# Moving the output projection of a Mamba-2 chunk behind the next chunk's head loop

## The chip, the cores and the metric

The program runs on all 8 cores of one Trainium2 chip. Each core computes half of one of four sequences, and the cores exchange nothing. The metric is the device time of the slowest core in microseconds (us); lower is better. Engines are named as in the profile: PE is TensorE (its matmuls; PEld its weight loads), DVE is VectorE, ACT is ScalarE, POOL is GpSimd and SP is SyncE. A "q" behind a name (POOLq) stands for the part of an engine that issues DMA transfers. TensorE's clock has two levels, 1.2 and 2.4 GHz; the profile prints the granted clock as 0.50 and 1.00.

## The reference

One transformer layer on `x` of shape (4, 4096, 1024): a layernorm, then a Mamba-2 block with a gated feed-forward network behind it, and beside them a second feed-forward network with integer weights, all added to `x`. What matters here is the Mamba-2 mixer and its output projection:

```python
def step(h, inputs):
    dA_t, dt_t, B_t, x_t, C_t = inputs
    dBx = jnp.einsum('bh,bn,bhp->bhpn', dt_t, B_t, x_t)
    h = h * dA_t[:, :, None, None] + dBx
    y = jnp.einsum('bhpn,bn->bhp', h, C_t)
    return (h, y)
_, ys = jax.lax.scan(step, h0, (tm(dA), tm(dt), tm(Bm), tm(x), tm(Cm)))
y = jnp.moveaxis(ys, 0, 1) + D[None, None, :, None] * x
y = y.reshape(b, l, D_INNER)
y = rmsnorm(y * jax.nn.silu(z), ssm_norm_w)
return jnp.einsum('ble,de->bld', y, out_proj_w)
```

There are 32 heads of 64 columns (2048 in all) and a state of 128.

## The kernel before

Each core works through its 2048 tokens in phases, with a barrier between them. Phase A normalises and transposes the tokens. `phase_B` projects and convolves. `phase_C` is the state recurrence in chunks of 128 tokens. It runs twice: `phase_C(1)` carries the state over the preceding half of the sequence and gives no output; `phase_C(0)` does the core's own half and is where the change acts. Phases E and F are the two feed-forward networks.

The order of the work is the order in which `self.op` is called: each call appends one instruction to the list of its engine, with the semaphore values that it waits for. An engine works its list in order, so an instruction that waits holds up everything behind it on the same engine. Semaphores are counted: `sv` by DVE, `st` by PE, `sa` by ACT and `sg` by POOL.

In `phase_C(0)` the 16 rounds of the loop over `ch` (line 792) do this:

- `stageA(ch + 1)` and `bcast_chain(ch + 1)` prepare the decay factors of the next chunk. The chain writes them to device memory and reads them back, spread over all partitions, on SP's queue.
- Sixteen transposes bring x to `x_tok`, and one brings B to `B_tok` (lines 807 to 815). PE transposes, and DVE copies out.
- `vxw` (line 816), on DVE, scales `x_tok` into `xw`.
- `emit_tail(ch - 1)` (line 820) is the output projection of the chunk before. It is 32 matmuls of 128x512 from `ynT` and `wout` into the PSUM tile P1 (line 689), then on DVE the addition of the residual, `h_t<-P,xn_t` (line 697, `ev_o`), and on POOL the transfer of the result to device memory (line 703).
- `mg` and `Gm` (lines 822 and 828) and the `zmm` matmuls (line 833) with `ez`, `y_acc<-P,pt` (line 840), begin the chunk's own output.
- The head loop (lines 846 to 881) does for each of 32 heads a DVE subtraction (`Est`, 855), an ACT exponential (861), a DVE product (`Emt`, 870) and one PE matmul of 64 columns (876) into P0.
- `ev_y` (line 883) adds P0 to `y_acc` on DVE. `tD` (line 886) is the product D * x on POOL, `cscr<-x_tok,c_dexp`; its results are added to `y_acc` by `ev_y2` (line 890) on DVE.
- The state update follows: four matmuls into P0 (line 905, `smm`), `c1` (914) and `t_carry` (919) on DVE. POOL fetches `sz_t` (line 924). Then come the gate (930), the norm (935 to 944) and sixteen transposes of `yn` to `ynT` (line 949), which the next tail reads.

The last chunk's tail is emitted behind the loop, at line 959. One detail of the order carries weight below: POOL's list in a round is the transfer of line 703, then `tD`, then the transfer of line 924. The transfer at line 703 waits for `ev_o`:

```python
t_h1_sp[cc] = self.op("gpsimd", ..., wait=[("sv", ev_o)], ...)
tD = self.op("gpsimd", ..., wait=[("sv", t_xtok), ("sa", t_endB[ch - 1][1])], ...)
ev_y2 = self.op("vector", ..., wait=[("sv", ev_y), ("sg", tD)], ...)
```

Of the kernel before, what the change touches and what calls it, by code (L numbers as in the profile page):

```python
# [55 lines left out]
def ts(i, n=128):  # L56
    return slice(i * n, (i + 1) * n)


class B:  # L60
# [542 lines left out]
    def phase_C(self, stream):  # L603
        import os as _os
        pre = stream == 1
# [69 lines left out]
        t_p0v = None  # L675
# [5 lines left out]
        pend_tail = {}  # L681

        def emit_tail(cc):
            nonlocal t_xn_pv
            ynt_c, ldxn_c = pend_tail.pop(cc)
            omm_c = None
            for f in range(16):
                for q in range(2):
                    omm_c = self.op("tensor", lambda e, f=f, q=q: e.matmul(  # L689
                        P1[:, q * 512:(q + 1) * 512], ynT[:, f * 128:(f + 1) * 128],  # L690
                        wout[:, f * DM + q * 512:f * DM + (q + 1) * 512],
                        start=(f == 0), stop=(f == 15)),
                        wait=([("sv", ynt_c), ("dw", self.t_wo),
                               ("sv", t_xn_pv)]
                              if f == 0 and q == 0 else []),
                        inc=("st", 1) if f == 15 and q == 1 else None)
            ev_o = self.op("vector", lambda e: e.tensor_tensor(
                h1_t[:, :], P1[:, 0:1024], xn_t[:, :], ALU.add),
                wait=[("st", omm_c), ("dh%d" % (cc % 2), ldxn_c),
                      ("dn%d" % ((cc - 1) % 2), t_h1_sp.get(cc - 1))],  # L700
                inc=("sv", 1))
            t_xn_pv = ev_o
            t_h1_sp[cc] = self.op("gpsimd", lambda e, cc=cc: e.dma_start(
                self.h1_dram[ts(cc), :], h1_t[:, :]),
                wait=[("sv", ev_o)], inc=("dn%d" % (cc % 2), 16))
# [86 lines left out]
        for ch in range(NCH):  # L792
# [14 lines left out]
            for f in range(16):  # L807
# [8 lines left out]
            vxw = self.op("vector", lambda e, dw=dw_: e.tensor_tensor(  # L816
                xw[:, :], x_tok[:, :], exp64(dw), ALU.mult),
                wait=[("sv", A["vdw"]), ("sv", t_btok)], inc=("sv", 1))
            if not pre and (ch - 1) in pend_tail:
                emit_tail(ch - 1)  # L820
            if not pre:
                mg = self.op("tensor", lambda e, W0=W0: e.matmul(
                    slotB_f[:, 0:128], xbc[:, 16 * CW + 3 + W0:16 * CW + 3 + W0 + Q],
# [22 lines left out]
                for hh in range(NH + 2):  # L846
# [18 lines left out]
                    if hh >= 2:  # L865
# [14 lines left out]
                                                 if h == 0 else []),  # L880
                            inc=("st", 1))
                t_mt_last = t_mth[NH - 1]
                ev_y = self.op("vector", lambda e: e.tensor_tensor(
                    y_acc[:, :], y_acc[:, :], P0[:, :], ALU.add),
                    wait=[("st", t_mt_last), ("sv", ez)], inc=("sv", 1))
# [7 lines left out]
                t_ya = ev_y2  # L893
                if self.dev_phase is not None:
# [5 lines left out]
                    t_ya = ("so", tdmp)  # L900
            else:
                t_ya = None
            smm = None
            for q in range(4):
                smm = self.op("tensor", lambda e, q=q: e.matmul(
                    P0[:, q * 512:(q + 1) * 512], B_tok[:, :],
                    xw[:, q * 512:(q + 1) * 512], start=True, stop=True),
                    wait=([("sv", vxw)] +
                          ([(t_ya if isinstance(t_ya, tuple) else ("sv", t_ya))]
                           if not pre else [("sv", t_p0v)])  # L910
                          ) if q == 0 else [],
                    inc=("st", 1) if q == 3 else None)
            t_smm = smm
# [8 lines left out]
            t_p0v = t_carry  # L922
# [488 lines left out]
```

How the kernel before makes its waits and increments, by code:

```python
        def run(e, fn=fn, waits=waits, inc=inc):  # L103
            for sn, v in waits:
                e.wait_ge(sems[sn], v)
            inst = fn(e)
            if inc is not None and inst is not None:
                inst.then_inc(sems[inc[0]], inc[1])
# [3 lines left out]
    def wait(self, eng, semname, val):  # L112
        if val:
            sems = self.sems
            self.emits[eng].append(lambda e, sn=semname, v=val: e.wait_ge(sems[sn], v))
```

## Time and profile before

| what | us |
| --- | --- |
| time of the kernel, median of 2 runs | 4405.84 |
| the two runs | 4354.16 and 4457.51 |
| the profiled execution's own time | 4357.55 |
| its span, slowest core (core 2) | 4356.0 |
| spans of all cores | 4345.9 to 4356.0 |
| DVE busy over the span | 1838.4 (42%) |
| PE busy over the span | 2288.3 (53%) |
| POOL busy over the span | 155.6 (4%) |

The profiled execution is one run; its time and its span differ by 1.6 us, so work outside the span plays no part. All durations below come from this execution, on core 2. Rows of the timeline give the start in us, the length in us, the engine, the line and the operation as out<-in; in brackets stands how long the engine was idle before it, and whose result ended that idle time.

### The profile page before, as it was taken

Reading aid. Unit: us, or ns where it says so; the run is one execution under the profiler, and the core shown is the slowest. Engines: PE = TensorE matmul, PEld = TensorE weight load, DVE = VectorE, ACT = ScalarE, POOL = GpSimd, SP = SyncE. Lnnn points to the kernel's source line nnn. Section 1 sums busy time; section 2 is a strip of 40 time slices with the busy share of each in tenths; the row PEclk is TensorE's granted clock in tenths of the full one; section 3 lists DMA queues with packets and bytes.
Section 4 is the critical chain, followed back from the end, with each engine's and each line's share of the span. In section 5 each row is a group of like instructions: output and inputs, shape, how many; then the busy total and the mean of one; then the engine's idle time right before and its main releaser. Section 6 shows DMA issues by size and latency. Waiting matters only on the chain.

```text
span 4356.0 us, 36502 instructions; the slowest of 8 cores (4345.9 to 4356.0 us)
## 1 busy us (share of the span) xinstructions
PE 2288.3 (53%) x9681; PEld 1024.3 (24%) x9681; DVE 1838.4 (42%) x3928; ACT 557.7 (13%) x1011; POOL 155.6 (4%) x160
## 2 busy tenths in 40 slices
PE   0536323435664334343434334777767746788777
PEld 0212111212222111121111111333333313333333
DVE  3533675655515576767666641222222201222222
ACT  3000110000113121212121210111111100000000
POOL 0110000000010000000000000000000000000000
PEclk9998665557877555555555557788887878889988
DMA  6552100011031411111111138000000093111111
GB/s 169 186 162 65 28 0 1 1 38 26 1 77 39 92 64 39 64 44 59 49 54 49 54 70 134 20 20 20 20 20 20 15 151 76 34 34 51 34 34 37
DMA packets 94289, 234.09 MB, mean 54 GB/s; under 512 B 23984, under 2 KB 26832, under 8 KB 93456
## 3 DMA queue, kind: packets, MB, share of 16 engines
q0 software_dynamic: 40448, 106.44, 11.1%
q1 hardware_dynamic: 51344, 116.94, 8.7%
q10 hardware_dynamic: 2304, 8.39, 0.5%
q8 instruction: 91, 1.49, 0.1%
q14 instruction: 102, 0.84, 0.1%
HBM read 235.13 MB, written 51.66 MB: 66 GB/s over the span
## 4 chain that ended last, share of the span: by engine, by line
PE 44%; DVE 23%; issue 14%; DMA 12%; ACT 5%; DVEq 1%; another core or an unknown queue 1%; SPq 0%; ACTq 0%; POOL 0%; POOLq 0%
PE P L1083 4%; PE P L1246 4%; PE P L1250 4%; PE P L689 3%; PE P L478 3%; PE P L483 3%; PE P L1087 3%; DVE Emt L870 3%; DMA bcast<-lam_dram 2%; PE P L1286 2%; PE PS L659 2%; PE P L1125 2%; PE PS L1286 2%; PE PS L1125 2%; DMA wbuf<-w_in 2%
## 5 line engine op out<-in xcount | busy, mean ns | idle before, releaser
L876 PE MATMUL P<-x_tok,Emt 128*128 128x64 bf16 x512 | 108.4, 212 | 328.9 <-DVE Emt L870 328.1
L430 DVE SCALAR_TENSOR_TENSOR B_acc<-xbc,c_convw,B_acc 128x2048 bf16<-128x2048 bf16 x108 | 245.3, 2345 | 0.0
L861 ACT ACTIVATE Est<-Est 128x128 f32<-128x128 f32 x512 | 155.6, 309 | 521.6 <-DVE Est L855 520.1
L1268 DVE TENSOR_TENSOR F_h<-F_h,P 128x1024 bf16<-128x1024 bf16 x48 | 58.6, 1221 | 386.9 <-ACT F_h L1262 386.9
L1105 DVE TENSOR_TENSOR E_h<-E_h,P 128x1024 bf16<-128x1024 bf16 (+1 forms) x48 | 53.3, 1110 | 383.6 <-ACT E_h L1099 383.6
L855 DVE TENSOR_SCALAR Est<-bcast,lam_tok 128x128 f32<-128x128 f32 x512 | 184.8, 366 | 52.1 <-DMA bcast<-lam_dram 2.1
L332 PE MATMUL P<-c_identf,A_n 128*128 128x128 f32 x256 | 90.5, 445 | 196.7 <-DVE A_n L320 165.0
L1246 PE MATMUL P<-wg,F_xf 128*128 128x512 bf16 x384 | 149.1, 388 | 84.1 <-ACT F_h L1262 42.1
L478 PE MATMUL P<-xfh,wbuf 128*128 128x512 bf16 x288 | 115.0, 399 | 144.9 <-DVE wbuf L454 125.6
L1083 PE MATMUL P<-wg,E_hnT 128*128 128x512 bf16 x384 | 146.6, 405 | 82.2 <-ACT E_h L1099 61.3
L870 DVE SCALAR_TENSOR_TENSOR Emt<-Est,dtk,Gm 128x128 bf16<-128x128 f32 x512 | 175.8, 346 | 8.2 <-PE P L876 5.9
L492 DVE TENSOR_TENSOR xbc<-P,r1bc 128x1024 bf16<-128x1024 f32 x72 | 88.3, 1227 | 201.9 <-PE P L483 201.9
L478 PE MATMUL P<-xf,wbuf 128*128 128x512 bf16 x288 | 112.1, 389 | 109.5 <-DVE wbuf L454 109.5
L1125 PE MATMUL P<-wd,E_h2t 128*128 128x512 bf16 x352 | 152.9, 434 | 19.0 <-DMA wd<-w_d 10.2
L1286 PE MATMUL P<-wd,F_h3t 128*128 128x512 bf16 x336 | 146.0, 435 | 27.1 <-DMA wd2b<-w_d 18.4
L1246 PE MATMUL P<-wu,F_xf 128*128 128x512 bf16 x384 | 149.3, 389 | 20.5 <-DMA wu<-w_u 20.5
L1083 PE MATMUL P<-wu,E_hnT 128*128 128x512 bf16 x384 | 140.6, 389 | 23.3 <-DMA wu<-w_u 23.3
L1262 ACT ACTIVATE F_h<-P 128x1024 bf16<-128x1024 f32 x48 | 49.2, 1024 | 805.4 <-PE P L1250 805.4
L1125 PE MATMUL PS<-wd,E_h2t 128*128 128x512 bf16 x352 | 152.1, 432 | 0.0
L1250 PE MATMUL P<-wu,F_xf 128*128 128x512 bf16 x384 | 149.1, 388 | 0.0
L1250 PE MATMUL P<-wg,F_xf 128*128 128x512 bf16 x384 | 149.1, 388 | 0.0
L876 PEld LDWEIGHTS P<-x_tok,Emt 128*128 128x128 bf16 x512 | 53.3, 104 | 390.2 <-issue 390.2
(197 smaller groups left out, 4286.1 us busy)
## 6 DMA issues: line engine op xcount, KB each, us to landing
bcast<-lam_dram SPq DMA_DIRECT2D x64, 512.0 KB
A_x<-x_own SPq DMA_DIRECT2D x32, 512.0 KB, 4.2
A_x<-x_pre SPq DMA_DIRECT2D x32, 512.0 KB, 4.1
wd<-w_d POOLq DMA_DIRECT2D x2, 5376.0 KB, 65.3
wg<-w_g POOLq DMA_DIRECT2D x5, 2048.0 KB, 43.7
wu<-w_u POOLq DMA_DIRECT2D x5, 2048.0 KB, 49.7
xn_dram<-A_n POOLq DMA_DIRECT2D x16, 512.0 KB, 4.8
xfh<-xfp_dram SPq DMA_DIRECT2D x4, 2048.0 KB, 14.2
```

The costliest lines, as they stand in the source:

```text
L430: e.scalar_tensor_tensor(a[:, :], xbc[:, ec * CW + k:ec * CW + k + T], self.c["convw"][:, ec * 4 + k:ec * 4 + k + 1], a[:, :], ALU.mult, A ...
L478: [e.matmul(sl[:, 0:512], self.wbuf[:, dc * 1184 + cr: dc * 1184 + cr + 128], r[:, 0:512], start=(dc == 0), stop=(dc == NDC - 1)), e.matmu ...
L483: e.matmul(sl[:, 512:1024], self.wbuf[:, dc * 1184 + cr: dc * 1184 + cr + 128], r[:, 512:1024], start=(dc == 0), stop=(dc == NDC - 1))][-1],
L855: e.tensor_scalar(est[q3][:, :], bc[g % 2][:, (h % 8) * 128:(h % 8 + 1) * 128], lt[:, h:h + 1], CLAMP, ALU.subtract, ALU.min),
L861: t_ee[h] = self.op("scalar", lambda e, q3=q3: e.activation(est[q3][:, :], est[q3][:, :], AF.Exp), wait=[("sq", gq + 1) if lastg else ("sv ...
L870: e.scalar_tensor_tensor(emt[q][:, :], est[q3][:, :], dk[:, h:h + 1], Gm[:, :], ALU.mult, ALU.mult),
L876: t_mth[h] = self.op("tensor", lambda e, h=h, q=q: e.matmul(P0[:, h * 64:(h + 1) * 64], emt[q][:, :], x_tok[:, h * 64:(h + 1) * 64], start ...
L1083: e.matmul(slots[j][:, 0:512], hnTt[p][:, dc * 128:(dc + 1) * 128], w[:, dc * INTER1 + cb:dc * INTER1 + cb + min(cn, 512)], start=(dc == 0 ...
L1125: mm = self.op("tensor", lambda e, k=k, q=q, pb=pb, kp=kp: e.matmul(pb[:, 0:512], h2t[0:kp, k * 128:(k + 1) * 128], wd1[0:kp, k * DM + q * ...
L1246: e.matmul(slots[j][:, 0:512], xft[p][:, dc * 128:(dc + 1) * 128], w[:, dc * INTER2 + cb:dc * INTER2 + cb + 512], start=(dc == 0), stop=(d ...
L1250: e.matmul(slots[j][:, 512:1024], xft[p][:, dc * 128:(dc + 1) * 128], w[:, dc * INTER2 + cb + 512:dc * INTER2 + cb + 1024], start=(dc == 0 ...
L1286: wt=wsrc[0], kk=wsrc[1]: e.matmul(pb[:, 0:512], h3t[:, k * 128:(k + 1) * 128], wt[:, kk * DM + q * 512:kk * DM + (q + 1) * 512], start=(k ...
```

## The change

It does two things in `phase_C(0)`.

1. The call of `emit_tail(ch - 1)` goes from its place behind `vxw` to behind the head loop, just ahead of `ev_y`. This concerns 15 of the 16 tails; the last one stands behind the loop as before.
2. The four `smm` matmuls wait for `ev_y` in place of `ev_y2`.

Nothing else is edited. Line numbers fall by two behind the first place, are the old ones again from `ev_y` (883) on, and fall by one behind line 905.

```diff
@@ -816,8 +816,6 @@
             vxw = self.op("vector", lambda e, dw=dw_: e.tensor_tensor(
                 xw[:, :], x_tok[:, :], exp64(dw), ALU.mult),
                 wait=[("sv", A["vdw"]), ("sv", t_btok)], inc=("sv", 1))
-            if not pre and (ch - 1) in pend_tail:
-                emit_tail(ch - 1)
             if not pre:
@@ -880,6 +878,8 @@
                 t_mt_last = t_mth[NH - 1]
+                if (ch - 1) in pend_tail:
+                    emit_tail(ch - 1)
                 ev_y = self.op("vector", lambda e: e.tensor_tensor(
                     y_acc[:, :], y_acc[:, :], P0[:, :], ALU.add),
                     wait=[("st", t_mt_last), ("sv", ez)], inc=("sv", 1))
@@ -906,8 +906,7 @@
                     wait=([("sv", vxw)] +
-                          ([(t_ya if isinstance(t_ya, tuple) else ("sv", t_ya))]
-                           if not pre else [("sv", t_p0v)])
+                          ([("sv", ev_y)] if not pre else [("sv", t_p0v)])
                           ) if q == 0 else [],
```

On DVE, between the transposes of a chunk and its head loop, this stood before (`x_tok`, `B_tok` and `xw` are the chunk's inputs, `h_t` is the tail's addition, the numbers behind names are buffers):

```order
L663 COPY B_tok<-PT 128x128
L816 TENSOR_TENSOR xw<-x_tok,dtw_70 128x2048
L697 TENSOR_TENSOR h_t<-P,xn_t 128x1024
L828 TENSOR_TENSOR Gm<-PT,c_triu_b 128x128
L840 TENSOR_TENSOR y_acc<-P,pt_72 128x2048
L855 TENSOR_SCALAR Est_104<-bcast_102,lam_tok_62 128x128
```

And at the same place on DVE in the changed kernel:

```order
L663 COPY B_tok<-PT 128x128
L816 TENSOR_TENSOR xw<-x_tok,dtw_71 128x2048
L826 TENSOR_TENSOR Gm<-PT,c_triu_b 128x128
L838 TENSOR_TENSOR y_acc<-P,pt_73 128x2048
L853 TENSOR_SCALAR Est_104<-bcast_102,lam_tok_63 128x128
```

The tail's addition is gone from here, and `Gm` follows `xw` directly. It now stands on DVE at the end of the head loop, between the last `Emt` and `ev_y`:

```order
L868 SCALAR_TENSOR_TENSOR Emt_108<-Est_105,dtk_74,Gm 128x128
L697 TENSOR_TENSOR h_t<-P,xn_t 128x1024
L883 TENSOR_TENSOR y_acc<-y_acc,P 128x2048
L890 TENSOR_TENSOR y_acc<-y_acc,cscr 128x2048
L913 TENSOR_TENSOR cscr<-Hst,gam_66 128x2048
L918 TENSOR_TENSOR Hst<-cscr,P 128x2048
L929 TENSOR_TENSOR y_acc<-y_acc,sz_t 128x2048
```

`ev_y` and all that comes behind it on DVE now stand behind an instruction that waits for the 32 matmuls. On PE, at the end of the head loop, the changed kernel has these 32 matmuls between the last head (line 874) and the state update:

```order
L874 MATMUL P<-x_tok,Emt_107 128x64
L874 MATMUL P<-x_tok,Emt_108 128x64
L689 MATMUL P<-wout,ynT 128x512 x32
L905 MATMUL P<-xw,B_tok 128x512 x4
L659 MATMUL PS<-c_ident,yn 128x128
```

Before, the 32 stood ahead of the chunk's `mg` (line 822), and line 905 came directly behind the last head. On POOL the changed kernel's list reads, in each chunk:

```order
L703 DMA h_dram<-h_t 128x1024
L886 TENSOR_TENSOR cscr<-x_tok,c_dexp 128x2048
L923 DMA sz_t<-sz_dram 128x2048
```

This is the same list as before. Nothing moved on POOL, but the first of the three waits for the tail's addition, which now comes at the other end of the head loop.

## Rows read from the trace of the kernel before

**Rows 1.** Span and mean granted clock of the slowest core
```profile
core 2: 4356.0 us, clock 0.733
```

**Rows 2.** Waits, 1511 to 2594 us: total us, times, longest us
```profile
DVE h_t L697 <- PE PT L822: 97.3, 15, 7.1
...
PE P L905 <- DVE y_acc L890: 76.1, 15, 5.1
```

**Rows 3.** Timeline, one chunk from the tail into the head loop
```profile
2012.46 8.86 PE L689 MATMUL P<-wout,ynT 128*128 128x512 bf16 x32
2012.78 2.29 DVE L816 TENSOR_TENSOR xw<-x_tok,dtw 128x2048 bf16<-128x2048 bf16 x1
...
2021.56 1.23 DVE L697 TENSOR_TENSOR h_t<-P,xn_t 128x1024 f32<-128x1024 f32 x1 [6.49 <-PE PT L822]
2022.70 0.28 DVE L828 TENSOR_TENSOR Gm<-PT,c_triu_b 128x128 bf16<-128x128 f32 x1
2022.90 2.28 DVE L840 TENSOR_TENSOR y_acc<-P,pt 128x2048 f32<-128x2048 f32 x1
2023.34 0.54 POOL L703 DMA_DIRECT2D h_dram<-h_t  x1 [66.48 <-DVE Gm L828]
2023.89 4.06 POOL L886 TENSOR_TENSOR cscr<-x_tok,c_dexp 128x2048 f32<-128x2048 bf16 x1
2025.10 3.41 DVE L855 TENSOR_SCALAR Est<-bcast,lam_tok 128x128 f32<-128x128 f32 x3
2027.89 0.59 POOL L924 DMA_DIRECT2D sz_t<-sz_dram  x1
...
2028.63 0.35 DVE L870 SCALAR_TENSOR_TENSOR Emt<-Est,dtk,Gm 128x128 bf16<-128x128 f32 x1
```

**Rows 4.** Timeline, the same chunk from its last head on
```profile
2049.28 0.21 PE L876 MATMUL P<-x_tok,Emt 128*128 128x64 bf16 x1 [0.34 <-DVE Emt L870]
2049.67 2.29 DVE L883 TENSOR_TENSOR y_acc<-y_acc,P 128x2048 f32<-128x2048 f32 x1 [0.53 <-PE P L876]
2052.13 2.29 DVE L890 TENSOR_TENSOR y_acc<-y_acc,cscr 128x2048 f32<-128x2048 f32 x1 [0.17 <-DVE y_acc L883]
...
2054.57 1.87 PE L905 MATMUL P<-xw,B_tok 128*128 128x512 bf16 x4 [5.08 <-DVE y_acc L890]
...
2056.93 2.29 DVE L919 TENSOR_TENSOR Hst<-cscr,P 128x2048 f32<-128x2048 f32 x1
2059.13 2.28 DVE L930 TENSOR_TENSOR y_acc<-y_acc,sz_t 128x2048 f32<-128x2048 f32 x1
```

**Rows 5.** Timeline, chunk 0, which has no tail ahead of its head loop
```profile
1445.54 4.04 POOL L886 TENSOR_TENSOR cscr<-x_tok,c_dexp 128x2048 f32<-128x2048 bf16 x1 [18.98 <-DVE x_tok L663]
...
1446.23 5.50 DVE L816 TENSOR_TENSOR xw<-x_tok,dtw 128x2048 bf16<-128x2048 bf16 x1
...
1451.65 0.28 DVE L828 TENSOR_TENSOR Gm<-PT,c_triu_b 128x128 bf16<-128x128 f32 x1
1451.85 2.27 DVE L840 TENSOR_TENSOR y_acc<-P,pt 128x2048 f32<-128x2048 f32 x1
...
1454.89 0.35 DVE L870 SCALAR_TENSOR_TENSOR Emt<-Est,dtk,Gm 128x128 bf16<-128x128 f32 x1 [0.18 <-ACT Est L861]
```

**Rows 6.** Windows: from:to us, length, busy us (count) by engine, granted clock (PEclk), DMA
```profile
2012.40:2016.00 3.60, 3.54 (x9) 1.31 (x10) 2.52 (x2) 0.00 (x0) 0.00 (x0) 0.50 0.00 0
2016.00:2021.20 5.20, 5.20 (x26) 2.30 (x24) 0.00 (x0) 0.00 (x0) 0.00 (x0) 0.99 0.00 0
...
2026.00:2048.00 22.00, 6.14 (x29) 3.01 (x29) 18.49 (x62) 9.42 (x31) 2.48 (x2) 0.51 0.29 97
```

**Rows 7.** Line 924, from issue of the transfer to its landing
```profile
DMA to landing us min/median/max: 3.5/3.9/10.7
```

**Rows 8.** Timeline, weight loads of line 905 at the low clock
```profile
2054.95 0.15 PEld L905 LDWEIGHTS P<-xw,B_tok 128*128 128x128 bf16 x1 [0.28 <-issue]
2055.38 0.15 PEld L905 LDWEIGHTS P<-xw,B_tok 128*128 128x128 bf16 x1 [0.28 <-issue]
```

## The prediction

> **What bounds the kernel now.** I read the span of the cores first: 4356.0 us on the slowest, beside an own time of 4357.55 [rows 1]. Next I read the waits of the second recurrence phase. One wait of DVE belongs to the change: the tail's addition (line 697) stands idle for 97.3 us in 15 chunks, 6.49 us in each [rows 2]. Its releaser is printed as the transpose slot of line 822; that matmul is only the next on PE behind the 32 matmuls of the tail, so the tail is what ends the wait. Then I followed one chunk on the timeline [rows 3, 4]. The reader is to see that DVE sets the pace on both sides of the head loop: `xw`, the wait for the tail, `h_t`, `Gm`, `y_acc`, then the heads, then five operations of 2.3 us each, one behind the other. PE and POOL matter only where DVE waits for them. So the sum is kept on DVE: what each place adds to or takes from its chain, per chunk, times 15. Chunk 0 has no tail ahead of its heads and shows what the freed place looks like [rows 5]; it stays as it is, and so does the last tail behind the loop.
>
> **A, the old place (a gain).** From the end of `xw` (2012.78 + 2.29 = 2015.07) to the start of `Gm` (2022.70) pass 7.63 us [rows 3]: 6.49 idle and 1.14 from the addition's start to the next. In chunk 0 `xw` ends at 1451.73 and `Gm` starts at 1451.65, 0.08 earlier [rows 5]. Gain 7.71 us. `Gm` and `y_acc` need their matmuls (lines 822 and 833), five in all; without the tail they run while DVE is in `xw`, as in chunk 0, so nothing new is late here.
>
> **B, the start of the head loop (a gain).** From the start of `y_acc` at line 840 to the first `Emt` pass 5.73 us in the chunk shown (2022.90 to 2028.63) and 3.04 in chunk 0 (1451.85 to 1454.89) [rows 3, 5]. The difference lies in the first three `Est`, which take 3.41 us together and end just after POOL's product D * x (2023.89 + 4.06 = 2027.95) [rows 3]. In chunk 0 the product runs beside `xw`, and there `xw` takes 5.50 us in place of 2.29 [rows 5, 3]: some DVE operations stand still until POOL's ends, while `y_acc`, which reads PSUM, takes 2.28 beside it as without it [rows 3, 5]. With the change the product leaves the head loop (see D). Gain 2.69 us.
>
> The Trainium skill (SBUF — State Buffer, section "SBUF: two separate sides") says that VectorE and GpSimd share a port pair that one instruction holds to its end, against VectorE operations in a two-port mode or with two SBUF inputs. By that rule the trace agrees: 5.50 against 2.29 us for `xw`, and an unhindered 2.28 for `y_acc` with its PSUM input. Without the rule B would be 0, which is a rival below.
>
> **C, the new place (a cost).** `ev_y` starts 0.39 us after the start of the last head's matmul now (2049.28 to 2049.67) [rows 4]. In the changed kernel PE goes from that matmul to the 32 of the tail, and DVE has nothing to do meanwhile but to wait, since `h_t` stands ahead of `ev_y` in its list. The step to the first of the 32 lies between 0 and the 0.21 us of the head's matmul; I take 0.1. From the first of the 32 to the start of `h_t` pass 9.10 us (2012.46 to 2021.56), and 1.14 more to the next DVE operation [rows 3]. That is 10.34 in place of 0.39: a cost of 9.95 us. The 2.3 us of cover that `xw` gave the tail is lost; that is why the same wait comes back longer than it was.
>
> The 9.10 us hold 3.6 us at a granted clock of 0.50 (1.2 GHz) and then about 1.0 (2.4 GHz) [rows 6]. The tail of now starts at the low level, behind the transposes, and the head loop's 22 us are at 0.51 as well [rows 6], so the new tail starts at the same level. I keep 9.10. The longest of the 15 idle times is 7.1 against the mean of 6.49 [rows 2], so 0.6 us per tail either way is an ordinary spread: 9 us in all. The far bound is a tail at the low level throughout: a matmul each 0.43 us [rows 8] gives 32 x 0.43 = 13.8 us.
>
> The Trainium skill (TensorE: Matmul & The Clock Gate, section "What's actually happening") says that the throttled state is the default and activity releases it. The rows agree in that both the transposes and the heads leave the clock at 0.50 and the dense run lifts it. By that rule the 32 matmuls lift it in the new place too, and the sum is as I have it.
>
> **D, the product on POOL (a cost that the diff doesn't show).** POOL's list is as before, but its first entry, the transfer of line 703, waits for `h_t`. The product stands behind it, and `ev_y2` waits for the product. Counted from the start of `h_t`: the transfer begins after 1.78 us (2023.34), the product after 2.33 (2023.89), and it ends after 6.39 (2027.95) [rows 3]. DVE takes some 0.15 to wake (its own hand-over at line 890 took 0.17 [rows 4]): `ev_y2` at 6.54. Without the wait `ev_y` would start after 1.14, and `ev_y2` 2.46 later (2049.67 to 2052.13) [rows 4]: at 3.60. Cost 2.94 us. Now the product hides in the head loop; its cover is gone. `ev_y` reads PSUM, so by B's rows it isn't slowed beside the product. The bounds of D are 0, if the product were done in time, and 4.06, its whole length.
>
> Queued behind the product is `sz_t` (line 924). It is issued as the product ends, 6.33 us after the start of `h_t` (2027.89), and lands 3.9 us later [rows 3, 7], at 10.2. The gate at line 930 needs it 7.00 us after `ev_y2` starts (2052.13 to 2059.13) [rows 4], at 13.5. That leaves 3.3 us, so it costs nothing. The transfer of `xn_t` for the next tail comes almost a chunk early.
>
> **E, the earlier wait of `smm`.** Its four matmuls wait for `ev_y2` now, 5.1 us in each chunk [rows 2]. But they run 2054.57 to 2056.44, beside `c1`, and line 919, which needs them, starts at 2056.93 when `c1` is done [rows 4]. The wait was hidden. With the edit they run beside `ev_y2` or its wait: worth 0, between 0 and the 0.1 us in which DVE passes from one to the next.
>
> **Sum.** Costs 9.95 + 2.94 = 12.89; gains 7.71 + 2.69 = 10.40; net 2.49 us slower per chunk, x 15 = 37 us. On the profiled execution's own 4357.55 that is 4395 us, 0.9% more. The median shown, 4405.84, is the middle of two runs, 4354.16 and 4457.51; the profiled execution lies at the faster, and my number is of that kind. About 2%, or 87 us, is what a measurement of this kernel can tell from no change.
>
> **The rivals.**
> 1. The product stays hidden, and the kernel isn't slower. If POOL had the product done by the time `ev_y` ends, D would be 0 and the sum -0.45 per chunk: 4351 us. For it: the product's inputs are ready a whole head loop earlier, and POOL was idle for 66.48 us [rows 3]. Against it: POOL takes its list in order and the transfer ahead of it waits for `h_t`. It decides if the product ends over 2.5 us sooner than I count.
> 2. The clock stays low, and the kernel is slower by over 2%. The heads leave PE with 6.14 us of work in 22 [rows 6], less than transposes do. If the tail then ran at the low level to its end it would take 4.7 us more, 15 x 4.7 = 70: 4465 us. It decides from a tail of some 12.4 us on, where 15 x 3.3 brings the loss to 87. Against it: 9 matmuls at the low level sufficed before [rows 6].
> 3. `sz_t` is late. With the longest landing seen, 10.7 us [rows 7], it would be there at 17.0 and the gate wait 3.5 us: 15 x 3.5 = 52, 4447 us, 2.1% slower. Against it: the median is 3.9, and it needs over 7.2 to cost anything.
> 4. B isn't paid back, because the first `Est` are slow for another reason than the product (a transfer, say). Then 40 us are missing: 4435 us. Against it: three `Est` end with the product, and chunk 0 has them fast.
>
> **How the numbers follow.** I give the forecast 0.68, and the rivals 0.12, 0.06, 0.08 and 0.06. The range runs from 4345, rival 1 less the spread of the tails, to 4450, which takes in rivals 3 and 4; only a tail at the low level lies outside. Faster by over 2% needs 87 us, more than any case gives: 0.02. Slower by over 2% is rival 2 and about half of rival 3, with a little for two costs at once: 0.12. The rest, 0.86, is within 2%.
>
> **What would show it.** In the changed profile the wait of `h_t` should be for line 689 and about 9.2 us (15 times, some 140 us in all), with no idle time between `xw` and `Gm`. The first three `Est` should take 0.7 to 0.9 us. `ev_y2` should show a new wait of 2.9 us on POOL, and the chunk should have grown by 2.5 us. I am wrong if a tail takes over 12 us, if the wait for POOL is missing, if `Est` stays at 3.4, or if a wait on `sz_t` shows at the gate.

## The result, and the profile after

The changed kernel is slower by 1.1%: the ratio of its time to the time before is 1.011, with a 95% interval of 1.0057 to 1.0163. Its profiled execution took 4412.81 us against 4357.55, 55.3 us more. The median over all its runs, 4441.53 us, and the 4359.99 of the kernel before hold runs in which one die's clock was lower, so the ratio, which leaves these out, and the two profiled executions are what the text compares.

The spans of the changed kernel's cores, beside [rows 1]:

```profile
core 0: 4411.2 us, clock 0.725
...
die 0 (median of its cores): 4395.2 us, clock 0.725
die 1 (median of its cores): 4400.4 us, clock 0.727
```

The old place, in one chunk on core 0, beside [rows 3] (start us, length us, engine, line, operation):

```profile
2040.15 2.29 DVE L816 TENSOR_TENSOR xw<-x_tok,dtw 128x2048 bf16<-128x2048 bf16 x1
...
2042.35 0.28 DVE L826 TENSOR_TENSOR Gm<-PT,c_triu_b 128x128 bf16<-128x128 f32 x1
2042.63 2.29 DVE L838 TENSOR_TENSOR y_acc<-P,pt 128x2048 f32<-128x2048 f32 x1
2044.84 0.67 DVE L853 TENSOR_SCALAR Est<-bcast,lam_tok 128x128 f32<-128x128 f32 x3
2045.69 0.35 DVE L868 SCALAR_TENSOR_TENSOR Emt<-Est,dtk,Gm 128x128 bf16<-128x128 f32 x1 [0.18 <-ACT Est L859]
```

`Gm` follows `xw` with no idle time, and the first three `Est` take 0.67 us in place of 3.41. Both gains are there. The new place, the same chunk, beside [rows 4]:

```profile
2066.64 0.21 PE L874 MATMUL P<-x_tok,Emt 128*128 128x64 bf16 x1 [0.34 <-DVE Emt L868]
2066.98 9.21 PE L689 MATMUL P<-wout,ynT 128*128 128x512 bf16 x31
...
2076.44 1.23 DVE L697 TENSOR_TENSOR h_t<-P,xn_t 128x1024 f32<-128x1024 f32 x1 [9.95 <-PE P L689]
2077.58 2.28 DVE L883 TENSOR_TENSOR y_acc<-y_acc,P 128x2048 f32<-128x2048 f32 x1
2078.22 0.54 POOL L703 DMA_DIRECT2D h_dram<-h_t  x1 [70.16 <-DVE h_t L697]
2078.77 4.07 POOL L886 TENSOR_TENSOR cscr<-x_tok,c_dexp 128x2048 f32<-128x2048 bf16 x1
2080.00 1.02 PE L905 MATMUL P<-xw,B_tok 128*128 128x512 bf16 x4 [3.81 <-DVE y_acc L883]
2082.77 0.59 POOL L923 DMA_DIRECT2D sz_t<-sz_dram  x1
2082.93 2.29 DVE L890 TENSOR_TENSOR y_acc<-y_acc,cscr 128x2048 f32<-128x2048 f32 x1 [3.08 <-POOL cscr L886]
2085.33 2.29 DVE L913 TENSOR_TENSOR cscr<-Hst,gam 128x2048 f32<-128x2048 f32 x1
2087.73 2.29 DVE L918 TENSOR_TENSOR Hst<-cscr,P 128x2048 f32<-128x2048 f32 x1
2089.93 2.28 DVE L929 TENSOR_TENSOR y_acc<-y_acc,sz_t 128x2048 f32<-128x2048 f32 x1
```

TensorE's clock over the last heads and over the two parts of this tail (from:to us, length, then busy us and counts of PE, PEld, DVE, ACT and POOL, the granted clock, and DMA):

```profile
2050.00:2066.00 16.00, 5.05 (x24) 2.51 (x24) 13.03 (x47) 7.23 (x24) 0.00 (x0) 0.50 0.27 101
2067.00:2071.70 4.70, 4.70 (x12) 1.65 (x13) 0.00 (x0) 0.00 (x0) 0.00 (x0) 0.54 0.19 68
2071.70:2076.60 4.90, 4.44 (x20) 1.86 (x19) 0.16 (x1) 0.00 (x0) 0.00 (x0) 1.00 0.00 0
```

DVE now stands idle for 9.95 us ahead of `h_t`, and for 3.08 us ahead of line 890, where the profile names POOL's product. From `ev_y2` to the gate pass 7.00 us (2082.93 to 2089.93) as before, so neither `sz_t` nor the state matmuls hold anything. The waits of the phase in sum (total us, times, longest), beside [rows 2]:

```profile
DVE h_t L697 <- PE P L689: 162.6, 16, 10.5
...
PE P L905 <- DVE y_acc L883: 57.1, 15, 3.8
DVE y_acc L890 <- POOL cscr L886: 46.4, 15, 3.3
```

The 16 waits of `h_t` include the last tail behind the loop; before, the 15 inner ones were 97.3 us. Worked out from the starts of these DVE operations on core 0 of either trace, as means over chunks 1 to 14:

| place on DVE | before | changed | difference | forecast |
| --- | --- | --- | --- | --- |
| A: start of `xw` to start of `Gm` | 9.87 | 2.21 | -7.66 | -7.71 |
| B: start of `y_acc` to first `Emt` | 5.73 | 3.06 | -2.67 | -2.69 |
| head loop, first to last `Emt` | 20.07 | 20.17 | +0.10 | 0 |
| C: last `Emt` to start of `ev_y` | 0.88 | 11.61 | +10.73 | +9.95 |
| D: start of `ev_y` to `ev_y2` | 2.46 | 5.37 | +2.91 | +2.94 |
| a whole chunk, `xw` to `xw` | 71.27 | 74.80 | +3.53 | +2.49 |

15 x 3.53 is 53 us of the 55. (The five places add up to 3.41; the last 0.1 lies between the start of `Gm` and the start of `y_acc`, 0.31 us in place of 0.20, and its cause is open.)

### The profile page after: what moved, and what is told of

Its sections match the earlier page's. It is cut to its first block, busy times and chain, and to the rows that moved or that the text cites. A ratio compares the mean times of both kernels' runs of the same rounds, so it can differ in the third digit from the quotient of the medians.

```text
span 4411.2 us, 36332 instructions; the slowest of 8 cores (4390.3 to 4411.2 us)
## 1 busy us (share of the span) xinstructions
PE 2286.5 (52%) x9511; PEld 1027.3 (23%) x9681; DVE 1797.2 (41%) x3928; ACT 556.8 (13%) x1011; POOL 156.1 (4%) x160
## 4 chain that ended last, share of the span: by engine, by line
PE 42%; DVE 20%; issue 16%; DMA 12%; ACT 5%; POOL 2%; DVEq 1%; another core or an unknown queue 1%; SPq 0%; ACTq 0%; POOLq 0%
PE P L1249 4%; PE P L1082 4%; PE P L1245 4%; PE P L689 3%; PE P L1086 3%; PE P L478 3%; PE P L483 3%; DVE Emt L868 3%; DMA bcast<-lam_dram 2%; PE PS L1285 2%; PE PS L659 2%; PE PS L1124 2%; PE P L1285 2%; PE P L1124 2%; DMA wbuf<-w_in 2%
## 5 line engine op out<-in xcount | busy, mean ns | idle before, releaser
L659 PE MATMUL PS<-c_ident,yn 128*128 128x128 bf16 x128 | 33.9, 265 | 287.3 <-DVE yn L943 250.3
L868 DVE SCALAR_TENSOR_TENSOR Emt<-Est,dtk,Gm 128x128 bf16<-128x128 f32 x512 | 175.7, 346 | 10.2 <-PE P L874 7.0
L853 DVE TENSOR_SCALAR Est<-bcast,lam_tok 128x128 f32<-128x128 f32 x512 | 143.5, 285 | 53.2 <-DMA bcast<-lam_dram 3.4
L1285 PE MATMUL PS<-wd,F_h3t 128*128 128x512 bf16 x336 | 143.8, 428 | 29.7 <-DMA wd2b<-w_d 15.3
L689 PE MATMUL P<-wout,ynT 128*128 128x512 bf16 x496 | 150.0, 470 | 3.7 <-issue 0.9
```

The source lines that it names most:

```text
L689: omm_c = self.op("tensor", lambda e, f=f, q=q: e.matmul(P1[:, q * 512:(q + 1) * 512], ynT[:, f * 128:(f + 1) * 128], wout[:, f * DM + q * ...
L853: e.tensor_scalar(est[q3][:, :], bc[g % 2][:, (h % 8) * 128:(h % 8 + 1) * 128], lt[:, h:h + 1], CLAMP, ALU.subtract, ALU.min),
L868: e.scalar_tensor_tensor(emt[q][:, :], est[q3][:, :], dk[:, h:h + 1], Gm[:, :], ALU.mult, ALU.mult),
L1285: wt=wsrc[0], kk=wsrc[1]: e.matmul(pb[:, 0:512], h3t[:, k * 128:(k + 1) * 128], wt[:, kk * DM + q * 512:kk * DM + (q + 1) * 512], start=(k ...
```

## The experiments

Four kernels were run together first: each takes one part of the account away.

**tail_only and tail_only_2.** The move of the tail alone, with the second edit undone:

```diff
-                          ([("sv", ev_y)] if not pre else [("sv", t_p0v)])
+                          ([("sv", ev_y2)] if not pre else [("sv", t_p0v)])
```

> The changed kernel with its second edit undone: the tail stays behind the head loop, the four state matmuls wait for ev_y2 again. Theory (the whole loss comes from the move of the tail, the earlier wait of the state matmuls is worth nothing because they lie beside c1): the time of the changed kernel within 5 us, about 4413 us, the gate still 7.0 us behind the start of ev_y2. Rival (the earlier wait gives something back): slower than the changed kernel by up to 1.9 us in each of 16 chunks, 30 us, about 4443 us, with a new DVE wait at line 919.

Its six executions, 4483.52 to 4579.75 us, gave no ratio, so it was run again. In its profile a chunk took 74.63 us on core 0, and the gate started 7.00 us behind `ev_y2`, as expected.

> The same kernel as tail_only, once more, because its runs gave no comparison. Theory (the second edit is worth nothing): within 5 us of the changed kernel, ratio 1.011 to 1.012. Rival (it gives something back): up to 30 us slower than that, ratio 1.018.

The ratio of this run was 1.0114 (1.0096 to 1.0131), the median 4415.28 us, and a chunk on core 0 took 74.82 us against the changed kernel's 74.80. The rival's 1.018 is out. The earlier wait of the state matmuls is worth nothing: in the changed kernel they start 2.9 us before `ev_y2` does (2080.00 against 2082.93 above), and nobody was waiting for them.

**prod_first.** The changed kernel with POOL's product ahead of the tail's transfer in POOL's list:

```diff
+                tD = self.op("gpsimd", ..., wait=[("sv", t_xtok), ("sa", t_endB[ch - 1][1])], inc=("sg", 1))
                 if (ch - 1) in pend_tail:
                     emit_tail(ch - 1)
                 ev_y = ...
-                tD = self.op("gpsimd", ...)
```

> The changed kernel with POOL's product written ahead of the tail's transfer, its wait unchanged, so that it starts when x_tok is complete. Theory (the product blocks DVE operations that read two SBUF inputs): the 2.9 us wait of ev_y2 goes, but xw, beside which the product now runs, takes 5.5 us in place of 2.3 as in chunk 0, so 0.3 us per chunk slower than the changed kernel: about 4417 us. Rival (no blocking, the product is merely late in the changed kernel): xw stays at 2.3 us, 15 x 2.9 = 44 us faster, about 4369 us.

Ratio 1.0091 (1.0038 to 1.0144), the profiled execution at 4406.41 us. One chunk on the timeline:

```profile
2037.32 4.04 POOL L881 TENSOR_TENSOR cscr<-x_tok,c_dexp 128x2048 f32<-128x2048 bf16 x1 [32.59 <-DVE x_tok L663]
2037.95 5.55 DVE L816 TENSOR_TENSOR xw<-x_tok,dtw 128x2048 bf16<-128x2048 bf16 x1
```

The wait behind `ev_y` is gone (2.45 us from `ev_y` to `ev_y2`), and `xw` has taken its place with 5.55 us: it ends 2.14 us after the product (2041.36 to 2043.50), as if it had begun only then. Two costs of 3 us changed places, and a chunk stayed at 74.7 us. The rival's 4369 us is out. It came out 6 us faster than the changed kernel and not 4 slower; shorter tails, on which more below, are 0.27 x 15 = 4 us of that.

**prod_last_head.** The same, but the product waits for the last `Emt` of the loop, so that it falls into the time in which DVE waits for the tail:

```diff
+                tD = self.op("gpsimd", ..., wait=[("sv", vm), ("sa", t_endB[ch - 1][1])], inc=("sg", 1))
                 if (ch - 1) in pend_tail:
                     emit_tail(ch - 1)
                 ev_y = ...
-                tD = self.op("gpsimd", ...)
```

> The changed kernel with POOL's product written ahead of the tail's transfer and waiting for the last Emt of the head loop, so that it runs while DVE waits for the tail's 32 matmuls. Theory (of the chunk's growth, 2.9 us are the wait for the product): that wait goes, xw stays at 2.3, the first Est stay fast, 15 x 2.9 = 44 us faster than the changed kernel: about 4369 us, some 5 to 12 us above the kernel before, which is what the longer, uncovered wait for the tail costs beyond the two gains. Rival (the product's wait hides another one, such as sz_t or the state matmuls): no more than half of it comes back, 4390 us or above, and the new wait shows behind ev_y2.

Ratio 0.9979 (0.9924 to 1.0033), the profiled execution at 4356.83 us: the whole loss is gone. The timeline shows the product beside the tail's matmuls, and `ev_y2` with no more than its own hand-over:

```profile
2039.27 4.04 POOL L881 TENSOR_TENSOR cscr<-x_tok,c_dexp 128x2048 f32<-128x2048 bf16 x1 [59.94 <-DVE Emt L868]
2039.58 8.59 PE L689 MATMUL P<-wout,ynT 128*128 128x512 bf16 x32 [0.15 <-issue]
...
2048.41 1.23 DVE L697 TENSOR_TENSOR h_t<-P,xn_t 128x1024 f32<-128x1024 f32 x1 [9.34 <-PE P L689]
2049.55 2.28 DVE L887 TENSOR_TENSOR y_acc<-y_acc,P 128x2048 f32<-128x2048 f32 x1
2050.18 0.60 POOL L703 DMA_DIRECT2D h_dram<-h_t  x1 [6.86 <-DVE h_t L697]
...
2052.00 2.29 DVE L890 TENSOR_TENSOR y_acc<-y_acc,cscr 128x2048 f32<-128x2048 f32 x1 [0.17 <-DVE y_acc L887]
```

It gave back 56 us where 44 were expected. The 2.9 us per chunk of the product are 44 of them; 0.5 us per chunk, 7 in all, are a shorter tail, which was not expected. In the trace a chunk is 3.43 us shorter, 51 in all; the last 5 us are within what single executions differ by.

**before_prod_xw.** The kernel before, its tail at the old place, and only the product moved, into the wait for the tail there:

```diff
             vxw = ...
+            if not pre:
+                tD = self.op("gpsimd", ..., wait=[("sv", vxw), ("sa", t_endB[ch - 1][1])], inc=("sg", 1))
             if not pre and (ch - 1) in pend_tail:
                 emit_tail(ch - 1)
...
                 ev_y = ...
-                tD = self.op("gpsimd", ...)
```

> The kernel before, the tail at its old place, with POOL's product written ahead of the tail's transfer and waiting for xw, so that it runs while DVE waits for the tail. Theory (B: the product blocks the first Est of the head loop): the first three Est fall from 3.4 to 0.7 us, 2.7 us in each of 15 chunks, 40 us faster than before, about 4317 us, ratio 0.991. In chunk 0, too, xw falls from 5.5 to 2.3. Rival (the first Est are slow for another reason): no change, 4357 us. It also shows whether the tail's low-clock stretch of 3.6 us depends on what runs before it or on the length of the chunk: behind the transposes, with a chunk of 69 us, it stays at 3.6 us if the first, and spreads between 2.3 and 5.7 if the second.

The ratio is 0.9887, but its interval, 0.9722 to 1.0051, reaches past 1, so the time alone doesn't settle it; the trace does. From `y_acc` to the first `Emt` pass 3.05 us in place of 5.73, `xw` of chunk 0 takes 2.29 in place of 5.50, and a chunk on core 0 takes 68.45 us in place of 71.27. Those 2.82 us are 42 in 15 chunks, where 40 were expected. B's mechanism holds in a kernel in which the tail hasn't moved. The expectation's last question, on the tail's low-clock stretch, is taken up under pad_long.

Two more kernels ask what a better placing would give, and what the clock costs.

**interleave.** The tail's matmuls are spread over the head loop, one behind each head, with its addition behind `ev_y` and the product as in prod_last_head:

```diff
                         t_mth[h] = self.op("tensor", ...)
+                        if (ch - 1) in pend_tail:
+                            omm = tail_mm(ch - 1, h // 2, h % 2)
                 t_mt_last = t_mth[NH - 1]
-                if (ch - 1) in pend_tail:
-                    emit_tail(ch - 1)
+                tD = self.op("gpsimd", ..., wait=[("sv", vm), ("sa", t_endB[ch - 1][1])], inc=("sg", 1))
                 ev_y = ...
-                tD = self.op("gpsimd", ...)
+                if (ch - 1) in pend_tail:
+                    emit_tail(ch - 1, omm)
```

> The tail's 32 matmuls one behind each head's matmul in the head loop, the tail's addition behind ev_y, and POOL's product waiting for the last Emt, ahead of the tail's transfer. Theory (the tail costs DVE only its wait, and PE has room beside the heads: a head comes each 0.65 us, its matmul and one of 128x512 take some 0.5 at the low clock): the head loop stays at 20.1 us, the wait of 6.5 us for the tail is gone, the first Est are fast, h_t and the end of the product cost 1.5 us behind ev_y. Per chunk 7.7 + 2.7 - 1.5 = 8.9 us less than before, 15 x 8.9 = 133 us: about 4224 us, ratio 0.969. Rival (the matmul in between delays each head's own, and the loop becomes bound by PE): the loop grows by up to 0.43 us per head, 13.8 us, and the kernel is slower than before.

Ratio 0.9705 (0.9686 to 0.9724), median 4237.27 us, the fastest of all: 2.95% below the kernel before. The heads on the timeline (DVE's `Emt`, the head's matmul at line 880, the tail's at 685), and the end of the loop:

```profile
2038.03 0.35 DVE L874 SCALAR_TENSOR_TENSOR Emt<-Est,dtk,Gm 128x128 bf16<-128x128 f32 x1
...
2038.52 0.21 PE L880 MATMUL P<-x_tok,Emt 128*128 128x64 bf16 x1
2038.55 0.61 PE L685 MATMUL P<-wout,ynT 128*128 128x512 bf16 x1
2038.68 0.35 DVE L874 SCALAR_TENSOR_TENSOR Emt<-Est,dtk,Gm 128x128 bf16<-128x128 f32 x1
```

```profile
1983.78 2.29 DVE L893 TENSOR_TENSOR y_acc<-y_acc,P 128x2048 f32<-128x2048 f32 x1 [0.68 <-PE P L880]
1985.99 1.22 DVE L703 TENSOR_TENSOR h_t<-P,xn_t 128x1024 f32<-128x1024 f32 x1
1987.47 2.29 DVE L898 TENSOR_TENSOR y_acc<-y_acc,cscr 128x2048 f32<-128x2048 f32 x1 [0.27 <-POOL cscr L889]
```

A head still comes each 0.65 us, the loop takes 20.17 us as in the changed kernel, `h_t` waits for nothing, and 0.27 us of the product show. A chunk takes 62.66 us, 8.6 less than before, where 8.9 were expected. The rival, a loop bound by PE, is out, though there isn't much room. PE is busy for 15.55 of 20 us in the loop shown, at a mean granted clock of 0.67. In 61 of the 112 loops of chunks 1 to 14 on the 8 cores the clock stays at 0.50 throughout. There PE is busy for 18.1 to 18.9 us, and the loop takes 20.18 us in the mean, as in the others.

```profile
2025.60:2045.60 20.00, 15.55 (x59) 4.31 (x60) 16.57 (x60) 9.18 (x31) 0.00 (x0) 0.67 0.24 80
...
2151.24:2171.42 20.18, 18.11 (x59) 4.48 (x61) 16.59 (x61) 9.20 (x31) 0.00 (x0) 0.50 0.23 80
```

Not all of the 8.6 us come from hiding the tail: before_prod_xw, which only moves the product, takes 2.8 us off a chunk. The other 5.8 us, 87 of the 129 in 15 chunks, are what spreading the tail adds to that.

**warm_fill.** The changed kernel with matmuls that are not part of the computation, to have PE busy ahead of the tail:

```diff
+                        if (ch - 1) in pend_tail and h >= 8:
+                            self.op("tensor", lambda e, W0=W0: e.matmul(
+                                P1[:, 0:512], xbc[:, 17 * CW + 3 + W0:17 * CW + 3 + W0 + Q],
+                                H_bf[:, 0:512], start=True, stop=True), ...)
                 t_mt_last = t_mth[NH - 1]
```

> The changed kernel with 24 matmuls of 128x512 that compute nothing needed, one behind the head matmul of each head from 8 on, into the P1 tile that the tail then overwrites. It is there to have TensorE busy ahead of the tail. Theory (the tail's 9.7 us hold some 4.7 at 1.2 GHz, which cost 2.4): the granted clock is 1.00 when the tail starts, the tail takes 7.1 us, 15 x 2.5 = 38 us faster than the changed kernel: about 4375 us. Rival (the tail's length isn't set by the clock at its start, but by weight loads or operands): the tail stays at 9.7 us and the time at 4413 us or above.

Ratio 1.0063 (1.0043 to 1.0083) beside 1.0114 of tail_only_2, run on the same chip: about 22 us faster, where 38 were expected. The mean of the tails fell from 9.6 to 7.9 us. Where the granted clock was at 1.00 from the start, a tail took 7.3 us, close to the 7.1 expected, but that was so in 27 of 112 tails. In 62 it rose only 1.3 to 3.0 us into the tail in spite of the filling. So the clock does set the length of the tail, and a filled PE doesn't make sure of it.

**pad_long and pad_short.** Why was the tail 9.6 us behind the heads and 9.1 behind the transposes? Two kernels leave everything ahead of the tail as it was and lengthen the chunk elsewhere, by doing `c1` twice (pad_long), or doing a quarter of it again (pad_short):

```diff
             c1 = ...
+            if not pre:
+                c1 = self.op("vector", lambda e, gm=gm_: e.tensor_tensor(
+                    cscr[:, :], H[:, :], exp64(gm), ALU.mult),
+                    wait=[("sv", c1)], inc=("sv", 1))
             t_carry = ...
```

> The kernel before with c1 done twice in each chunk of the second recurrence phase, which adds one DVE operation of 2.3 us, far from the tail and with nothing changed ahead of it. Question: why the tail ran 9.7 us in the changed kernel and 9.1 before. Theory (its low-clock stretch depends on how long a chunk is): it changes here too although the same transposes run ahead of the tail, to a mean of over 4.2 us from 3.7, and the tail to some 9.5 us. Rival (it depends on what TensorE did just before): it stays at 3.7 and the tail at 9.1. The time is 16 x 2.4 = 38 us longer by the rival, some 6 us more by the theory.

> As pad_long, with a quarter of the operation: some 0.65 us in each chunk. Theory (length of the chunk): the low-clock stretch changes, here to some 2.8 us, the tail is at 8.7 us in place of 9.1, so that two thirds of the added time are given back: 4 us in all in place of 10. Rival (what ran before): 3.7 us and 9.1, 10 us longer than before.

Each was executed once. pad_long took 4405.86 us beside 4365.61 of the kernel before on the same chip: 40 us more lie between the rival's 38 and the theory's 44, so this time doesn't decide, and the trace has to. Its wait for the tail rose from 97.3 us [rows 2] to 105.1:

```profile
its engine sat idle before it (us, times) until:
  PE PT L822: 105.1, 15
```

The low stretch, from the start of the tail to the rise of the granted clock, was 4.95 us in the mean, above the 4.2 that the theory asked for; the rival's 3.7 is out. In pad_short it was 4.0, not 2.8, and it went up and down between 2.6 and 5.9 from chunk to chunk: this expectation missed. pad_short's time, 4424.55 us, tells nothing of the pad, since its slowest core spent some 50 us more behind the phase, where nothing was changed. All kernels side by side, means over the tails of chunks 1 to 14 on all 8 cores, but for the chunk's length, which is that of core 0. "Low stretch" is the time from the tail's first matmul until the granted clock is 1.00, "tail" that from the first matmul to the start of `h_t`:

| kernel | ahead of the tail | chunk | low stretch | tail |
| --- | --- | --- | --- | --- |
| before | transposes | 71.3 | 3.8 | 9.20 |
| before_prod_xw | transposes | 68.5 | 3.5 | 9.05 |
| pad_short | transposes | 72.3 | 4.0 | 9.28 |
| pad_long | transposes | 74.6 | 5.0 | 9.74 |
| prod_last_head | heads | 71.4 | 3.7 | 9.13 |
| prod_first | heads | 74.7 | 4.2 | 9.37 |
| changed | heads | 74.8 | 4.7 | 9.64 |
| warm_fill | heads and filling | 73.2 | 1.2 | 7.94 |

In every row the tail is 7.3 us plus half of its low stretch, to within 0.1 us: that is what the lower clock costs.

Behind heads and behind transposes the mean stretch is the same where the chunk is as long (3.7 and 3.8 at 71.4 and 71.3 us), and it grows with the chunk behind either. So whether heads or transposes ran ahead of the tail isn't the cause. By what rule the length acts stays open. prod_first and the changed kernel differ by 0.5 us with chunks of one length, beside 1.2 us between the kernel before and pad_long. Single tails differ more than the means: in pad_long the stretch is 2.7 to 5.8 us. In before_prod_xw, whose expectation asked about this, the mean stayed near 3.6 as if what ran before decided it, but single tails went from 2.5 to 5.9 us (3.0 to 5.0 in the kernel before) as if the length did; that run alone settles nothing.

## Why the prediction was right or wrong

**The direction that was argued and the mechanism were right, the size was short.** The text forecast 37 us more than the profiled execution's own time, 0.9%; it became 55 us, and 1.1% by the ratio.

**A and B** came out within 0.05 us. prod_first and before_prod_xw show B's mechanism apart from the change: DVE operations with two SBUF inputs, or the `Est`, stand still beside POOL's product, and follow it wherever it is put. The rule of the Trainium skill that the forecast leaned on (SBUF — State Buffer, "SBUF: two separate sides") is borne out by 5.55 us for `xw` beside the product and 2.29 without. Rival 4, no payback of B, is out.

**D** was forecast at 2.94 us and measured 2.91; prod_last_head, which takes it away, brings the kernel back to the time before. Rival 1, the hidden product, was wrong of the changed kernel as written, and what it would have given, 4351 us, is about what prod_last_head measured with a product that really is hidden.

**C is the step that failed**, the term for the new place: 9.95 us forecast, 10.73 measured, 0.78 x 15 = 12 us of the 18 that were missing. That is 8% of the term, but the net is a small difference between large terms, and 0.78 us are over a fifth of the 3.53 us that a chunk grew by. Two parts of C were too small. "I take 0.1" for the step from the last head's matmul to the tail's first was 0.34 (2066.64 to 2066.98), longer than the 0.21 that I gave as the upper bound. And "I keep 9.10" for the tail was wrong by 0.5 us: the new tail does start at the low level, as argued, but its low stretch is 4.7 us in place of 3.8. I reasoned from what ran ahead of the tail. pad_long shows that a longer chunk lengthens the stretch with nothing changed ahead of the tail, and the change itself made the chunk longer. Length explains it only in part: prod_first, with a chunk as long, has 4.2 us, and what makes the other 0.5 us stays open. The rest is 0.1 us more in the head loop and 0.1 us more between `Gm` and `y_acc` in each chunk, and some 2 us outside the phase.

**Rivals 2 and 3** did not come. The longest wait of `h_t` is 10.5 us, short of a tail of 12.4, and the gate shows no wait for `sz_t`.

**E** was right: tail_only_2 and the changed kernel can't be told apart.

**The number on record was placed badly.** 4395 us was meant against 4357.55, but it lies below the 4405.84 that was shown as the time before, so that read against this it says "slightly faster", the opposite of the argument. The result is also clear of noise where the text counted about 2% as the least that can be told: its interval is half a percent to either side. The chance of 0.86 for "within 2%" was about the size of the loss and said nothing of its sign.

## What to carry to other kernels

Moving a block of matmuls doesn't hide it: what decides is which engine has work of its own in the new place, and here the old place had 2.3 us of cover and the new one none. Of the placings tried here, only spreading the block over a loop in which TensorE has gaps made its wait vanish (2% of the kernel's time, and another 1% came from placing the product better). When the gain is a difference of large terms, a small error in one of them is a large one in the answer: 8% of C was a fifth of the net. Read the whole list of every engine that the moved block issues to: an unmoved operation behind a moved wait moves too, and the GpSimd operation here cost nothing beside a wait of VectorE or beside an addition that reads PSUM (2.28 us with it, 2.29 without), and 3 us beside one that reads two SBUF tensors.

## What the runs showed of the hardware beyond that

The same 32 matmuls take 7.3 to 10.2 us, depending almost only on when the granted clock rises within them. In the mean that moment shifts with the length of the loop around them: lengthening each chunk by 2.4 us of unrelated DVE work made the tail 0.5 us longer on top (pad_long), and taking 2.9 us out of it made the tail 0.5 us shorter (prod_last_head). The shift isn't regular: pad_short added 0.8 us and moved the mean tail by under 0.1. A small edit anywhere in such a loop can thus have a second effect of up to some 0.5 us per round, 8 us in 15, either way.
